# The gate and up adapters' return product with packed rank rows

## What is computed

```python
def lora_add(base, inp, A, B):
    Ab = A[layer_idx][lora_indices]
    Bb = B[layer_idx][lora_indices]
    t = jnp.einsum('bri,bni->bnr', Ab, inp)
    return base + jnp.einsum('bor,bnr->bno', Bb, t) * SCALE     # rank 16, SCALE 0.5
gate = lora_add(jnp.einsum('bnh,fh->bnf', x, W_gate), x, A_gate, B_gate)
up = lora_add(jnp.einsum('bnh,fh->bnf', x, W_up), x, A_up, B_up)
act = jax.nn.silu(gate) * up
down = lora_add(jnp.einsum('bnf,hf->bnh', act, W_down), act, A_down, B_down)
```

## Time and profile before

| | us |
|---|---|
| runs before | 2086.11, 2084.29, 2087.57 |
| median | 2086.11 |
| span of the profiled execution | 2084.3 |
| TensorE busy | 2027.8 (97%) |
| VectorE busy | 1754.2 (84%) |
| ScalarE busy | 992.2 (48%) |
| mean traffic | 220 GB/s |

### The profile page before, as it was taken

The page is one execution under the profiler, slowest core; times in us unless marked ns, Lnnn a source line. Parts: engine busy times, 40 slices in busy tenths (PEclk is TensorE's granted clock), DMA queues, the critical chain, the costliest instruction groups (busy, mean ns, idle before and its releaser), DMA issues.

```text
span 2084.3 us, 33692 instructions
## 1 busy us (share of the span) xinstructions
PE 2027.8 (97%) x10192; PEld 1726.4 (83%) x10192; DVE 1754.2 (84%) x2204; ACT 992.2 (48%) x1255; POOL 135.2 (6%) x229
## 2 busy tenths in 40 slices
PE   3999999999999999999999999999999999999999
PEld 3998888878888788888888888888888888888887
DVE  8796999999999988778787779979788788767777
ACT  2222888878887533343343443453343343434332
POOL 3100000000000322210000020010000000000000
PEclk9999999999999999999999999999999999999999
DMA  6997999989999656754334996645334334368665
GB/s 246 336 343 282 353 352 359 359 339 352 359 354 340 168 164 198 196 143 109 91 101 114 341 316 210 205 144 129 94 101 110 91 106 106 96 215 306 198 209 187
DMA packets 247488, 459.51 MB, mean 220 GB/s; under 512 B 110534, under 2 KB 114822, under 8 KB 227718
## 3 DMA queue, kind: packets, MB, share of 16 engines
q1 hardware_dynamic: 230306, 416.03, 59.6%
q0 software_dynamic: 14944, 42.50, 6.7%
q10 hardware_dynamic: 2180, 0.26, 0.1%
HBM read 418.56 MB, written 63.73 MB: 231 GB/s over the span
## 4 chain that ended last, share of the span: by engine, by line
PE 86%; DVE 7%; issue 2%; DMA 2%; ACT 1%; POOLq 1%; DVEq 0%; POOL 0%; ACTq 0%; SPq 0%
PE ps L2323 19%; PE ps L2324 19%; PE ps L2325 19%; PE ps L2245 6%; PE ps L2247 6%; PE ps L2246 6%; PE ps L2217 5%; PE ps L2401 2%; PE ps L2402 2%; PE ps L2254 1%; DMA W<-in_w 1%; PE ps L2438 1%; PE ps L2439 1%; POOLq L750 1%; DVE part L1567 1%
## 5 line engine op out<-in xcount | busy, mean ns | idle before, releaser
L2323 PE MATMUL ps<-rows,oph 128*128 128x512 f32 x1196 | 467.3, 391 | 1.2 <-DVE opl L1659 0.6
L2324 PE MATMUL ps<-rows,oph 128*128 128x512 f32 x1196 | 466.9, 390 | 0.0
L2325 PE MATMUL ps<-rows,opl 128*128 128x512 f32 x1196 | 465.3, 389 | 0.0
L1567 DVE TENSOR_TENSOR part<-W,part 128x2048 fp32r<-128x2048 f32 x152 | 343.1, 2286 | 9.5 <-ACT part L919 8.9
L1662 DVE TENSOR_TENSOR tmp<-ps,tmp 128x512 f32<-128x512 f32 (+2 forms) x344 | 242.8, 707 | 106.9 <-PE ps L2402 61.4
L919 ACT ACTIVATE part<-W 128x2048 fp32r<-128x2048 f32 x152 | 290.6, 1915 | 70.8 <-DMA W<-in_w 47.9
L2325 PEld LDWEIGHTS ps<-rows,opl 128*128 128x128 f32 x1196 | 224.6, 188 | 47.7
L2323 PEld LDWEIGHTS ps<-rows,oph 128*128 128x128 f32 x1196 | 225.0, 188 | 45.6 <-DVE opl L1659 2.0
L2324 PEld LDWEIGHTS ps<-rows,oph 128*128 128x128 f32 x1196 | 225.0, 188 | 41.8
L2323 PE MATMUL ps<-th,wdh 128*128 128x512 f32 (+1 forms) x656 | 249.4, 380 | 1.5 <-DVE tl L1659 1.0
L2324 PE MATMUL ps<-tl,wdh 128*128 128x512 f32 (+1 forms) x656 | 248.7, 379 | 0.0
(11 more groups left out here) (246 smaller groups left out, 3028.0 us busy)
## 6 DMA issues: line engine op xcount, KB each, us to landing
W<-in_w SPq DMA_DIRECT2D x152, 1024.0 KB, 6.7
raw<-in_wgu SPq DMA_DIRECT2D x168, 256.0 KB, 2.8
traw<-kept_acts SPq DMA_DIRECT2D x78, 512.0 KB, 5.0
wraw<-in_wd SPq DMA_DIRECT2D x70, 512.0 KB
toep<-kpad SPq DMA_DIRECT2D x31, 1024.0 KB, 9.2
lraw<-picked_b SPq DMA_DIRECT2D x88, 256.0 KB, 4.1
kept_acts<-tmp SPq DMA_DIRECT2D x84, 256.0 KB, 2.4
urev<-in_urev SPq DMA_DIRECT2D x32, 256.0 KB, 7.1
```

Of the source, the lines that this page charges most:

```text
L1567: V.tensor_tensor(out=wl[c][:], in0=W[:, c], in1=wh[c][:].bitcast(F32), op=ALU.subtract).then_inc(w_lo, 1)
L2323: mm(to, lhsT=wh, rhs=mh, start=start, stop=False)
L2324: mm(to, lhsT=wh, rhs=ml, start=False, stop=False)
L2325: return mm(to, lhsT=wl, rhs=mh, start=False, stop=stop)
```

## The change

The ranks are packed otherwise. Of the 8 sequences of a tile, 128 rank rows in all, three overlapping spans of columns are formed: sequences 0 to 2 (192 columns), 5 to 7 (192) and 2 to 5 (256). A span's product carries several of the three terms for its sequences at once: its 128 partitions hold high and low rank rows together, in 48 + 48 + 32 (the ends) or 32 + 32 + 64 rows (the middle). `add_ranks` becomes three products of 192, 192 and 256 columns. In the one call that begins a bank (`start=True`, once per whole unit) the middle span is cut at the ends' limits into 64, 128 and 64 columns.

The right operand `tm` is made by TensorE: ScalarE and VectorE write high and low parts into `tt`, six products per tile with selection matrices `sel` (0 and 1) put the rows in their places in PSUM (`place_ranks`), and ScalarE copies them to `tm` (`ranks_placed`). The selection matrices are cut from the identity by 12 copies of GpSimd, behind the mask. `lraw` and `lt` hold 1536 instead of 1024 elements per partition, loaded by nine DMAs instead of two; `ranks_lo` becomes two instructions, on 32 and on 64 partitions. The scratch form of `lora_b` follows, the projection's raw data get a buffer of their own (`praw`), and `tml` with its clearing goes.

```diff
+SPANS = ((0, 3 * H), (5 * H, 8 * H), (2 * H, 6 * H))
+TERMS_AT = (0, 3 * H, 6 * H)
+RANK_ROWS = (((0, 0, 48), (48, 0, 48), (96, 0, 32)),
+             ((0, 80, 48), (48, 80, 48), (96, 96, 32)),
+             ((0, 48, 32), (32, 48, 32), (64, 32, 64)))
...
             def load_ranks(st, u):
-                src = lora_b[st, bass.ds(u, 1)].rearrange("a r g c w -> (a r) (g c w)")
-                for copy in range(2):
-                    sp.dma_start(lraw[copy * HALF:(copy + 1) * HALF].rearrange("p g c w -> p (g c w)"),
-                                 src).then_inc(lraw_in, 16)
+                for k, pieces in enumerate(RANK_ROWS):
+                    for to, at, n in pieces:
+                        src = lora_b[st, bass.ds(u, 1), at:at + n].rearrange("a r j w -> (a r) (j w)")
+                        sp.dma_start(lraw[to:to + n, k].rearrange("p j c w -> p (j c w)"), src).then_inc(lraw_in, 16)
...
             def clear(st):
-                pool.memset(tml[HALF:P].rearrange("p c g w -> p (c g w)").bitcast(F32), 0.0).then_inc(cleared, 1)
                 pool.memset(ahl[HALF:P].rearrange("p j h w -> p (j h w)").bitcast(F32), 0.0).then_inc(cleared, 1)
...
+            pool.wait_ge(mask_set, 4)
+            for k, pieces in enumerate(CHOSEN):
+                for to, at, n in pieces:
+                    last = pool.tensor_copy(sel[k][:, to:to + n], ident[:, at:at + n])
+            last.then_inc(sel_set, 1)
...
             def ranks_projected(st, j):
                 act.wait_ge(tm_part, st * 2 + j + 1)
-                for c in range(2):
-                    for dup in range(2):
-                        last = copy(tmh[dup * HALF:(dup + 1) * HALF, c, 2 * j:2 * j + 2].rearrange("p g w -> p (g w)"),
-                                    sraw[c * HALF:(c + 1) * HALF, 2 + j])
-                last.then_inc(tm_hi, 1)
+                copy(thl[j][0:HALF, 0], sraw[0:HALF, 2 + j])
+                copy(thl[j][0:HALF, 1], sraw[HALF:P, 2 + j])
+                copy(thl[j][HALF:P, 1], sraw[HALF:P, 2 + j]).then_inc(tm_hi, 1)
+
+            def ranks_placed(st, j):
+                act.wait_ge(placed_done, st * 2 + j + 1)
+                copy(tm[:, j, :, 0:2 * TERMS_AT[1]], ps[:, PLACE_BANK:PLACE_BANK + 2, 0:2 * TERMS_AT[1]])
+                copy(tm[:, j, :, TERMS_AT[2]:TERMS], bank(PLACE_REST).rearrange("p (c w) -> p c w", c=2)
+                     ).then_inc(tm_set, 1)
...
             def ranks_lo(st, u):
                 dve.wait_ge(lt_hi, u + (st * FT + 1))
-                sub(lt[HALF:P], lraw[HALF:P], lt[HALF:P].bitcast(F32)).then_inc(lt_lo, 1)
+                ends, rest = slice(96, P), slice(HALF, P)
+                sub(lt[ends, 0:2], lraw[ends, 0:2], lt[ends, 0:2].bitcast(F32))
+                sub(lt[rest, 2], lraw[rest, 2], lt[rest, 2].bitcast(F32)).then_inc(lt_lo, 1)
...
+            def place_ranks(st, j):
+                pe.wait_ge(tt_lo, st * 2 + j + 1)
+                if j:
+                    pe.wait_ge(tm_set, st * 2 + 1)
+                ends, rest = TERMS_AT[1], TERMS_AT[2]
+                for c in range(2):
+                    src = thl[j][:, c]
+                    mm(ps[:, PLACE_BANK + c, 0:ends], lhsT=sel[0], rhs=src[:, SPANS[0][0]:SPANS[0][1]], start=True, stop=True)
+                    mm(ps[:, PLACE_BANK + c, ends:rest], lhsT=sel[1], rhs=src[:, SPANS[1][0]:SPANS[1][1]], start=True, stop=True)
+                    last = mm(ps[:, PLACE_REST, c * GC:(c + 1) * GC], lhsT=sel[2], rhs=src[:, SPANS[2][0]:SPANS[2][1]],
+                              start=True, stop=True)
+                last.then_inc(placed_done, 1)

             def add_ranks(to, c, j, stop, start=False):
-                for g in (2 * j, 2 * j + 1):
-                    cols = slice(g % 2 * GC, (g % 2 + 1) * GC)
-                    mm(ps[:, to, cols], lhsT=lt[:, g, c], rhs=tmh[:, c, g], start=start and g % 2 == 0, stop=False)
-                    last = mm(ps[:, to, cols], lhsT=lt[:, g, c], rhs=tml[:, c, g], start=False,
-                              stop=stop and g % 2 == 1)
+                pieces = [(k, a, b) for k, (a, b) in enumerate(SPANS)]
+                if start:
+                    low, high = SPANS[0][1], SPANS[1][0]
+                    pieces[2:] = [(2, SPANS[2][0], low), (2, low, high), (2, high, SPANS[2][1])]
+                for n, (k, a, b) in enumerate(pieces):
+                    at = TERMS_AT[k] - SPANS[k][0]
+                    last = mm(ps[:, to, a:b], lhsT=lt[:, k, j, c], rhs=tm[:, j, c, at + a:at + b],
+                              start=start and n == 0, stop=stop and n == len(pieces) - 1)
                 return last
...
+            pe.wait_ge(sel_set, 1)
             for st in range(NST):
```

More of the change, by code:

```diff
@@ L259, in build @@
             ahl = sb(s, "ahl", [P, 2, 2, TILE], F32R)
-            lt = sb(s, "lt", [P, GR, 2, P], F32R)
+            lt = sb(s, "lt", [P, 3, 2, 2, P], F32R)
             adraw = sb(s, "adraw", [P, SEQ, R])
             adt = sb(s, "adt", [P, GR, P], F32R)
-        with placed(OPS_AT // 2, "tmh") as s:
-            tmh = sb(s, "tmh", [P, 2, GR, GC], F32R)
-            tml = sb(s, "tml", [P, 2, GR, GC], F32R)
+            tm = sb(s, "tm", [P, 2, 2, TERMS], F32R)
+            tt0 = sb(s, "tt0", [P, 2, TILE], F32R)
+            assert nc.sbuf_base <= floor + OPS_AT
         with placed(OPS_AT) as s:
@@ L290, in build @@
             tl1 = sb(s, "tl1", [P, 2 * TILE], F32R)
+        with placed(ROWS_AT + (14 * KH + 12) * TILE * 4 + 1024, "lraw") as s:
+            lraw = sb(s, "lraw", [P, 3, 2, 2, P])
+        with placed(ROWS_AT + (14 * KH + 16) * TILE * 4 + 1024, "sel2") as s:
+            sel_rest = sb(s, "sel_rest", [P, P], F32R)
+        with placed(ROWS_AT - GC * 4, "sel") as s:
+            sel_ends = sb(s, "sel_ends", [P, 2, P], F32R)
+        with placed(ROWS_AT + (14 * KH + 4) * TILE * 4, "tt1") as s:
+            tt1 = sb(s, "tt1", [P, 2, TILE], F32R)
+        thl = (tt0, tt1)
+        sel = (sel_ends[:, 0], sel_ends[:, 1], sel_rest[:])
         with placed(OPS_AT + 6 * TILE * 4, "traw2") as s:
@@ L769, in gather_outer @@
                 g, rows = s // GS, slice(s % GS * R, (s % GS + 1) * R)
-                pool.dma_start(lora_b[st, units, rows, g].rearrange("u r c w -> u r (c w)"),
+                mine = slice(s % TB * R, (s % TB + 1) * R)
+                pool.dma_start(lora_b[st, units, mine, s // TB],
                                ins["lora_b"][one, units].rearrange("a u r w -> (a u) r w")).then_inc(landed(st, units), 16)
@@ L1720, in ranks_cut @@
                 dve.wait_ge(tm_hi, st * 2 + j + 1)
-                for c in range(2):
-                    own = slice(c * HALF, (c + 1) * HALF)
-                    pair = lambda a: a[:, c, 2 * j:2 * j + 2].rearrange("p g w -> p (g w)")
-                    last = sub(pair(tml[0:HALF]), sraw[own, 2 + j], pair(tmh[own]).bitcast(F32))
-                last.then_inc(tm_lo, 1)
+                sub(thl[j][HALF:P, 0], sraw[0:HALF, 2 + j], thl[j][0:HALF, 0].bitcast(F32))
+                sub(thl[j][HALF:P, 1], sraw[HALF:P, 2 + j], thl[j][HALF:P, 1].bitcast(F32)).then_inc(tt_lo, 1)
             def ranks_lo(st, u):
                 dve.wait_ge(lt_hi, u + (st * FT + 1))
-                sub(lt[HALF:P], lraw[HALF:P], lt[HALF:P].bitcast(F32)).then_inc(lt_lo, 1)
+                ends, rest = slice(96, P), slice(HALF, P)
+                sub(lt[ends, 0:2], lraw[ends, 0:2], lt[ends, 0:2].bitcast(F32))
+                sub(lt[rest, 2], lraw[rest, 2], lt[rest, 2].bitcast(F32)).then_inc(lt_lo, 1)
             def down_ranks_lo(st, u):
```

61 lines of the change are left out of this document (41 added, 20 removed).

## The result

| | before | after |
|---|---|---|
| median of the runs, us | 2087.74 (8 runs) | 2098.61 (8 runs) |
| profiled span, us | 2084.3 | 2095.9 |
| TensorE busy, us | 2027.8 | 2018.3 |

The ratio is 1.0054, with a 95% interval from 1.0041 to 1.0067: the changed kernel is 0.5% slower. The forecast was 2085.3 us; the time lies 0.6 us above its range of 2068 to 2098.

A forecast was written before the change was run, and what follows sets the result against it. TensorE, busy 97% of the span, was taken as the bound. Terms -11.6 + 6.7 + 1.0 + 3.1 = -0.8 us on the profiled 2084.3 gave 2083.5, or 2085.3 as median (1.8 above); range 2068 to 2098.

The forecast's parts named there:

- The products: Rank products of the gate and up units: narrow ones cost 0.112 us each, the weight load's pace; gain 11.6 us.
- Time by columns: Rival for the narrow products: 192 columns cost 0.092 us, gain 27.1 us, 2070 us with the waits; chance 0.15.
- the F32 price: Rival for products below 256 columns: two passes, 0.32 us at 192 columns, +79.1 us, 2176 with the waits; chance 0.14.
- The start of the MLP: TensorE's first MLP product waits for the selection matrices and starts 6.4 us late; with the clock, +6.7 us.
- The third rival: Start of the MLP: late matrices and half clock, 3 to 5 us over 6.7; 2092 to 2096; chance 0.09, shared.
- The clock: Start of the MLP: about 2.0 us lost at half clock before would not be lost by a later full-clock start.
- Three times that stretch, the upper bound: Start of the MLP: clock at half for three times the earlier 3.4 us stretch, delay 9.0 us.
- a restart at full clock: Start of the MLP, the other bound: TensorE resumes at full clock after its wait, delay 4.4 us.
- The half unit of stage 0: Opening of stage 0: wait for ScalarE's lifting about 1.0 us, VectorE's longer lt chain late; +1.0 us (0.5 to 2.5).
- The half unit of stage 1: Opening of stage 1: cut, placing, lifting and first operand in a chain, first sums 2.55 us late; +3.1 us (2 to 6).
- Unit 21 and the down product: Stretch up to stage 1's second pair of projections: the prediction's terms sorted into it give -0.3 us.
- VectorE in the units and SP's loads: Steady units: VectorE's 0.6 us more fits its 4.3 spare, SP's loads some 4 us more per unit; costs nothing.

The follow-up runs named there:

- experiment 5: The changed kernel with TensorE's wait moved to the first placing, plus 804 more 192-column products in running banks: 2160.47 us in a single run.
- experiment 6: The changed kernel with one more wait, VectorE waiting for the selection matrices before its long row subtractions: 2089.04 us, ratio to before 1.0013.
- experiments 2: The changed kernel with the third selection matrix written by one copy of 128 columns instead of six: 2095.84 us, ratio to before 1.0043.
- Experiment 4: The changed kernel with TensorE's wait moved to the first placing and stage 1's half unit reordered on VectorE, ScalarE and TensorE: 2079.78 us, ratio to before 0.9967.
- experiment 3: The kernel before plus only the selection matrices' buffers, GpSimd's twelve copies and TensorE's wait for them: 2099.53 us, ratio to before 1.0060.
- experiment 1: The changed kernel with TensorE waiting for the selection matrices ahead of its first placing, not its first MLP product: 2083.35 us, ratio to before 0.9987.

## Why the prediction was wrong, point by point

- **The products: right.** 0.112 us each was taken from the weight loads of the earlier trace rows; 0.114 and 0.118 stand in the steady unit, 0.1085 to 0.112 in experiment 5. A unit should have taken 0.315 us less and takes 0.30 less. Time by columns and the F32 price are out.
- **The start of the MLP: the wait was foreseen, its length was not, and this is the step that failed.** That TensorE would stand for the matrices was forecast; that it would be 6.4 us late was not true: it was 13.5. The matrices should have been there 2.2 us after the mask's end and came 9.3 us after it (661.41 to 670.67). The copies were priced from the mask's COPY row, 0.73 us, scaled down to their columns, and 0.09 us fixed for each. As a price of GpSimd's own work that was not far off: with VectorE idle the twelve take 1.9 us (experiment 6). What the term put at nothing is GpSimd's wait for VectorE, 7.3 of the 9.2 us. The row was misread: its 0.73 was not GpSimd's time for 256 columns (that is 0.40, experiment 6) but was stretched by VectorE's instructions of 512 columns beside it. A duration that is the neighbour's does not scale with the row's own columns, and behind it VectorE had longer instructions in its queue. VectorE's timeline in the trace of before shows them, where I did not look for GpSimd's price:

```profile
663.29 2.28 DVE L1659 TENSOR_TENSOR rraw<-X 128x2048 f32<-128x2048 f32 x1
665.49 2.28 DVE L1659 TENSOR_TENSOR rows<-X,rows 128x2048 fp32r<-128x2048 f32 x1
```

  The third rival, set at 3 to 5 us more than the term and at a chance of 0.09 together with another case, had the place and the sign (a first product after 664; it came at 670.72) but not the size, 2092 to 2096 against 2098.6, and it put the excess down to late matrices and the clock, not to VectorE.
- **The clock.** It is at half from 657.70 to 674.75, where full speed returns; the window row (length, busy times, clock, DMA share, GB/s) is of its last part:

```profile
670.72:674.75 4.03, 4.03 (x19) 4.03 (x20) 0.00 (x0) 0.00 (x0) 0.00 (x0) 0.50 1.21 520
```

  4.0 us of products ran at half, against 3.4 in the kernel before. Three times that stretch, the upper bound, was not met; nor was the other bound, a restart at full clock. The 0.6 us more at half cost about 0.3 us, since at half clock a product of 256 columns starts every 0.21 us instead of 0.12.
- **The half unit of stage 0:** forecast +1.2 for the stretch to unit 3, measured +2.1, or +2.5 from the end of the second tile's projection, from which the prediction counts. TensorE's rows of after show a wait at the second placing that the forecast had not, the one for the lifting at 0.71 (forecast 1.0), and 1.74 at the wait for `lt` (the earlier trace rows had 1.02, and the forecast 1.6 more less 0.6):

```profile
701.69 0.36 PE L2451 MATMUL ps<-tt,sel_ends 128*128 128x192 f32 x1 [0.20 <-DVE tt L1702]
704.03 0.71 PE L2465 MATMUL ps<-tm,lt 128*128 128x192 f32 x4 [0.71 <-ACT tm L1017]
739.61 0.61 PE L2465 MATMUL ps<-tm,lt 128*128 128x192 f32 x3 [1.74 <-DVE lt L1702]
```

- **The half unit of stage 1:** forecast +3.3, measured +4.2. The order of the links is as forecast (cut, placing, lifting, first operand), and VectorE's first sum stands at 1416.57, which less the 13.04 us that this stage begins late is 0.9 later than forecast. That 0.9 comes from the sum itself. ScalarE's six copies were to be done at 1394.5, though four of them take 2.56 us in the earlier trace rows and six so 3.84; they begin at 1391.28 as forecast and end 0.6 later, at 1395.13. The rest is VectorE's cut, 1.39 us instead of 1.2, and short gaps:

```profile
1404.32 3.85 ACT L1017 ACTIVATE tt<-sraw 64x512 fp32r<-64x512 f32 x6 [3.02 <-DVE sraw L1708]
```

  The rank products at 1415.46 also run at half clock (1.65 us for six that take 0.84 otherwise), which was not in the term; but experiments 2 and 6 lose 3.6 and 4.0 us in this stretch without it. Experiment 4 shows that nearly all of it was the order of work, not the new work.
- **Unit 21 and the down product:** +0.6 against -0.3. TensorE's waits in it, all for VectorE, add to 2.0 us instead of 1.3. The other five kernels with the change and no further products lose 0.9 to 2.0 us there and experiment 3 nothing (-0.02), so it belongs to the packing and not to the copies; which link of the down product is late was not followed and stays open.
- **VectorE in the units and SP's loads: right at nothing.** VectorE is busy 18.4 of 21.6 us, and no steady unit waits.

## What to carry to other kernels

Before a duration is scaled, ask what ran beside it: a GpSimd copy next to a VectorE instruction that reads two operands from SBUF lasted as long as that instruction, so its row says nothing of its own width, and its price is the number of instructions times the length of the neighbour's. Put a wait at the instruction that needs the data, not ahead of the stage: here that one line was 13 us of 2098, more than the whole change could gain. Packing products narrower than 256 columns saves only down to the pace of the weight loads, so count products, not columns.

## What the runs showed of the hardware

- A GpSimd copy of 16 columns took 0.19 us alone and 2.25 us beside a VectorE subtraction of 2048 columns, one of 32 columns 0.20 beside a VectorE instruction with one of its operands in PSUM. Mask selections took 1.08 and 0.99 us beside VectorE's subtractions and 0.66 alone, and the subtractions beside them 1.14 and 1.13 instead of 0.69.
- Narrow products start as little as 0.05 us apart (64 columns, then 128), but the next wide product pays: 0.32 us to its successor instead of 0.23. Over groups of 3, 8 and 14 products with 64 to 256 columns the price is 0.112 to 0.118 us.
- After 14.2 us without work TensorE's clock stayed at half for 4.0 us of products in after and for 5.6 in experiment 3, and after 5.8 us without work for 6.2 in experiment 6: the longer wait did not cost more. After waits of 0.81 and 0.71 us, 2.3 us apart, it went to half as well, for some 3.5 us (1415.4 to 1418.9). In experiments 1, 2 and 6 it stayed at full speed behind the same two waits (0.81 and 0.71; in experiment 1 the window 1404.00 to 1408.00), and in experiment 1 it fell later, at 1439.7 behind a wait of 1.78. So these waits alone do not decide it:

```profile
1404.00:1408.00 4.00, 3.70 (x18) 2.93 (x18) 2.70 (x5) 1.84 (x4) 0.00 (x0) 1.00 0.22 63
```
